# A mixture of experts behind cross attention: expert tiles of 128 rows, each with its own expert, two to a group

## The chip, the cores and the metric

The kernel runs on one core of one Trainium2 chip. The metric is the time on the device in microseconds (us). TensorE's granted clock has two levels, 1.2 and 2.4 GHz; the profile shows it as 0.50 and 1.00. The profile's engines are PE (TensorE's matmuls), PEld (its weight loads), DVE, ACT, POOL and SP; a name with a q behind it (PEldq, SPq, ACTq, POOLq) is the engine's queue, its sequencer, which runs register instructions, waits and DMA issues. A read of a value from memory into a register is a TENSOR_LOAD there.

## The reference

The input is x, 32 x 256 tokens of 256 numbers (8192 tokens), and a context of the same shape, all in float32.

```
x = x + xattn(layernorm(x), ctx)          # 8 heads of 64, both directions, mixed by alpha
h = layernorm(x)                          # 8192 x 256
probs = softmax(h @ gate_w.T)             # 16 experts
w, idx = top_k(probs, 4); w /= sum(w)
g, u = h @ w1[e], h @ w3[e]               # 256 -> 128 each, per expert
y[e] = (silu(g) * u) @ w2[e]              # 128 -> 256
x = x + sum over the 4 chosen e of w[e] * y[e]
```

So 8192 x 4 = 32768 rows go through an expert, each through one of 16.

## The kernel before, in words

**Stage A** takes the 32 batches one after another: layer norm, projections, scores, softmax, attention, output projection, second layer norm, router. For each chosen expert of each token it sends the normed row by an indirect DMA of POOL into `x_rows`, a table in HBM with a region for each expert; behind the row's 256 numbers lies the row's place in the result `y_rows`. A matrix is held as a high and a low part, and each product is made of three passes (hi x hi, hi x lo, lo x hi: `PASSES`).

**The plan.** When the last batch is routed, DVE counts the rows of each expert (`count`), the groups that they fill (`over` is a comparison of 16 experts with `MOST` fill levels, `ngroups` its sum), and makes a table: for each group its row in `x_rows` and its expert. SP stores it and reads it back as `table_row`. SP and ACT write a pad behind each expert's rows, one group long, eight experts each (`pad_experts`, `pad`, lines 349 and 350): bias rows, and targets in a dump region behind `y_rows`. One more pad of one group for each of 16 unused groups is written in stage A.

**The expert stage** works on 144 groups of 256 rows (two tiles of 128 rows, n = 0 and 1, of the same expert). 144 is 32768 / 256 = 128 full groups and one partly filled for each of 16 experts. The order on each engine is written out by hand as a pipeline over the body of group j, r = j mod 8. The first and the last eight groups are unrolled, the rest is a loop whose body holds eight groups.

- SP (`load_group`, lines 419 and 420) reads the group's row from `table_row` into a register and loads 256 rows into one of eight buffers `xg`. For a buffer's next use it waits for the transposes of the group eight back, and for that group's sends.
- PE, in body j: reloads the expert of group j - 2 where r is 0 or 1 (the registers don't live across the loop's jump); transposes the rows of group j + 1 (line 1202, `p_xt`); reads the expert of j (line 1189); gate and up matmuls of j (line 1213, `p_gu`, 12 matmuls of 256 columns, whose weights are addressed by the expert's register); transposes the activations of j - 1 (line 1223, `p_at`); down matmuls of j - 2 (line 1231, `p_y`, 6 matmuls).
- ACT, in body j: tanh of j - 1 (line 663), copy of `p_at` of j - 2 (668), copy of `p_y` of j - 3 to `y_out` (673), copy of `p_xt` of j + 1 to `xgT_hi` (678). DVE does the products of silu (939, 942) and the low parts (948, 954).
- POOL sends the two tiles of `y_out` row by row to their places in `y_rows` by two indirect DMAs (line 524).

Two buffers lie between the steps (`p_xt`, `xgT`, `p_gu`, `gated`, `p_at`, `actT`, `p_y`), four for `y_out`, eight for `xg`. Line 43 is the helper that waits for a semaphore.

**The end**: when all sends have landed, SP loads the rows of `y_rows` and the residual, DVE weights and sums them, and ACT stores the result.

Of the kernel before, what the change touches and what calls it, by code (L numbers as in the profile page):

```python
# [6 lines left out]
F32 = mybir.dt.float32  # L7
F32R = mybir.dt.float32r
U32 = mybir.dt.uint32
I32 = mybir.dt.int32  # L10
# [5 lines left out]
P = 128  # L16
TOP_K = 4
# [10 lines left out]
def flat(ap):  # L28

    names = " ".join("abcd"[:len(ap.shape) - 1])  # L30
    return ap.rearrange(f"p {names} -> p ({names})")


def spread(ap, axis, shape):

    return ap.unsqueeze(axis).to_broadcast(shape)
# [9 lines left out]
def xattn_moe_kernel(nc, x, ctx, Wq1, Wk1, Wv1, Wq2, Wk2, Wv2, alpha_attn, Wout, bout,  # L46
# [12 lines left out]
    SCALE = HEAD_DIM ** -0.5  # L59
    TOKENS = B * S  # L60
    TT = TOKENS // P
    GROUP = 2 * P

    REGION = TOKENS + GROUP
    ROW = D + 4

    GROUPS = TOKENS * TOP_K // GROUP + E
    MOST = TOKENS // GROUP
    DUMP = TOKENS * TOP_K
    PIECE = KT * INNER  # L70
    LOADS = 8
    TC = -(-GROUPS // P)
    assert S == 2 * P and D == 2 * P and INNER == 4 * P and I == P and B >= 4 and B % 4 == 0
    assert math.frexp(SCALE)[0] == 0.5
    assert GROUPS % LOADS == 0 and GROUPS >= 3 * LOADS
    ROUTER_STEPS = 19

    x_rows = nc.dram_tensor("x_rows", [E * REGION + E * GROUP, ROW], F32, kind="Internal").ap()
    y_rows = nc.dram_tensor("y_rows", [DUMP + 2 * E * GROUP, D], F32, kind="Internal").ap()
    mid_rows = nc.dram_tensor("mid_rows", [TOKENS, D], F32, kind="Internal").ap()  # L80
    group_table = nc.dram_tensor("group_table", [2, TC * P], I32, kind="Internal").ap()

    with ExitStack() as stack:
        def sb(name, shape, dt=F32, stack=stack):
            return stack.enter_context(nc.sbuf_tensor(name, shape, dt))
# [32 lines left out]
        with ExitStack() as a:  # L118


            qT = [[sb(f"qT{d}_{part}", [P, PAIRS, S], F32R, a) for part in ("hi", "lo")] for d in range(2)]
            kT = [[sb(f"kT{d}_{part}", [P, PAIRS, S], F32R, a) for part in ("hi", "lo")] for d in range(2)]
            wp = [sb("wp_hi", [P, 6, KT, INNER], F32R, a), sb("wp_lo", [P, 6, KT, INNER], F32R, a)]
            gate_rows = sb("gate_rows", [E, D], stack=a)
            val = [sb(f"val{d}", [P, ST, INNER], stack=a) for d in range(2)]
            rows = sb("rows", [P, ST, D], stack=a)

            rowsT = [[sb(f"rowsT{i}_{part}", [P, KT, S], F32R, a) for part in ("hi", "lo")] for i in range(2)]
            x_in = sb("x_in", [P, ST, D], stack=a)
            x_res = sb("x_res", [P, ST, D], stack=a)  # L130
            x_mid = sb("x_mid", [P, ST, D], stack=a)
            probs = [sb(f"probs{i}", [P, 2, ST, S], stack=a) for i in range(2)]
            probsT = sb("probsT", [P, 2, ST, S], stack=a)
            attnT = sb("attnT", [P, PAIRS, S], stack=a)
            moeT = [sb("moeT_hi", [P, KT, S], F32R, a), sb("moeT_lo", [P, KT, S], F32R, a)]
            routed = sb("routed", [P, ST, TOP_K, ROW], stack=a)
            middle_slots = [sb(f"middle_slot{i}", [P, PIECE], stack=a)[:, :] for i in range(2)]
            pad_target = sb("pad_target", [P, 2 * E, 2], I32, a)
            small = lambda name, shape, dt=F32: sb(name, shape, dt, a)
            nmx, sums, inv = ([small(f"{n}{i}", [P, 4]) for i in range(2)] for n in ("nmx", "sums", "inv"))  # L140
            stats = small("stats", [P, ST, 6])
            mv = small("mv", [P, ST, 2])
            ve = small("ve", [P, ST])
            rstd = small("rstd", [P, ST])
            lmax = small("lmax", [P, ST])
            lexp = small("lexp", [P, ST, E])
            pexp = small("pexp", [P, ST, E])
            top = small("top", [P, ST, 8])
            topi = small("topi", [P, ST, 8], U32)
            topf = small("topf", [P, ST, TOP_K])  # L150
            tsum = small("tsum", [P, ST])
            trec = small("trec", [P, ST])
            onehot = small("onehot", [P, ST, TOP_K, E])
            chosen = small("chosen", [P, ST, E])
            chosen_b = small("chosen_b", [P, ST, E], BF16)
            place = small("place", [P, ST, E])
            slotf = small("slotf", [P, ST, TOP_K])
            slot_i = small("slot_i", [P, ST, TOP_K], I32)
# [184 lines left out]

            return not isinstance(j, int) or 0 <= j < GROUPS

        def pad(eng, row, n, groups):

            to = x_rows[bass.ds(row, groups * GROUP), :].rearrange("(n p) d -> p n d", p=P)
            eng.dma_start(to[:, :, 0:D], spread(bias[:, :], 1, [P, 2 * groups, D])).then_inc(pads_sent, 16)
            eng.dma_start(to[:, :, D:D + 1].bitcast(I32), flat(pad_target[:, n:n + groups, :]).unsqueeze(2),  # L350
                          allow_slow_non_contiguous=True).then_inc(pads_sent, 16)

        def pad_experts(eng, experts):
# [7 lines left out]
        def _(sp):  # L361
# [54 lines left out]
            sp.wait_ge(table_in, 16)  # L416

            def load_group(j, r):
                row = sp.value_load(table_row[0:1, 0, bass.ds(j, 1)], min_val=0, max_val=E * REGION + (E - 1) * GROUP)
                sp.dma_start(xg[r][:, :, 0:D + 1],  # L420
                             x_rows[bass.ds(row, GROUP), 0:D + 1].rearrange("(n p) d -> p n d", p=P)).then_inc(xg_in[r], 16)

            for r in range(LOADS):
                load_group(r, r)
# [24 lines left out]
        def _(pool):  # L449
            for t in (ident, before, ones, routed):  # L450
# [5 lines left out]

            pool.affine_select(out=before[:, :], in_=before[:, :], compare_op=ALU.is_gt, fill=0.0,
                               base=0, pattern=[[1, P]], channel_multiplier=-1).then_inc(consts_set, 1)
            pool.iota(pad_target[:, :, :], [[GROUP, 2 * E], [P, 2]], base=DUMP, channel_multiplier=1).then_inc(consts_set, 1)
            pool.memset(mhalf[:, :], -0.5).then_inc(consts_set, 1)  # L460
            for t, pattern, start, mult in (
                    (expert[:, :], [[1, E]], 0, 0),
                    (region[:, :], [[REGION, E]], 0, 0),
                    (base[:, :], [[REGION, E]], 0, 0),
                    (target[:, :, :], [[P * TOP_K, ST], [1, TOP_K]], 0, TOP_K),
                    (fills[:, :], [[GROUP, MOST]], 0, 0),
                    (tri[:, :, :], [[1, E], [-1, E]], 0, 0),
                    (group_no[:, :], [[P, TC]], 0, 1)):
                pool.iota(t, pattern, base=start, channel_multiplier=mult,
                          allow_small_or_imprecise_dtypes=True).then_inc(consts_set, 1)  # L470
# [225 lines left out]
        def _(dve):  # L696
# [205 lines left out]
            def planned(ins):  # L902
                n_steps[0] += 1
                ins.then_inc(plan_step, 1)
                dve.wait_ge(plan_step, n_steps[0])
# [14 lines left out]
            planned(dve.tensor_tensor(tstart[:, :], group_no[:, :], tstart[:, :], ALU.subtract))  # L920
            planned(dve.tensor_scalar(trow[:, :], texp[:, :], float(REGION), None, ALU.mult))
            planned(dve.tensor_copy(base_i[:, :], base[:, :]))
            planned(dve.scalar_tensor_tensor(trow[:, :], tstart[:, :], float(GROUP), trow[:, :], ALU.mult, ALU.add))

            dve.tensor_scalar(table[:, 1, :], texp[:, :], float(E - 1), None, ALU.min)
            planned(dve.tensor_copy(table[:, 0, :], trow[:, :]))
# [52 lines left out]
        def _(pe):  # L979
# [205 lines left out]
            pe.wait_ge(middle_hi, MIDDLE)  # L1185
            pe.wait_ge(late_lo, LATE)

            def expert_of(j):
                return pe.value_load(table_row[0:1, 1, bass.ds(j, 1)], min_val=0, max_val=E - 1)

            experts = {}

            def group(j, r):
                if exists(j - 2) and r < 2:
                    experts[(r - 2) % LOADS] = expert_of(j - 2)
                if exists(j + 1):
                    i = (r + 1) % 2
                    pe.wait_ge(xg_in[(r + 1) % LOADS], xg_loads(j + 1, r + 1))
# [4 lines left out]
                    mm.then_inc(xg_t, 1)  # L1203
                if exists(j):
                    i = r % 2
                    experts[r] = expert_of(j)
                    pe.wait_ge(xgT_lo, j + 1)
                    wait(pe, act_set, j - 1)
                    for n in range(2):
                        m = 0  # L1210
                        for k in range(KT):
                            for h, a in PASSES:
                                mm = pe.matmul(p_gu[:, i, n, :], xgT[i][h][:, n, k, :],  # L1213
                                               wgu[a][:, bass.ds(experts[r], 1), k, :, :].rearrange("p e g i -> p (e g i)"),
                                               start=(m == 0), stop=(m == 5))
                                m += 1
                    mm.then_inc(gu_done, 1)
# [7 lines left out]
                if exists(j - 2):  # L1225
                    i = r % 2
                    pe.wait_ge(actT_lo, j - 1)
                    wait(pe, y_set, j - 3)
                    for n in range(2):
                        for m, (h, a) in enumerate(PASSES):  # L1230
                            mm = pe.matmul(p_y[:, i, n, :], actT[i][h][:, n, :],  # L1231
                                           wdn[a][:, bass.ds(experts[(r - 2) % LOADS], 1), :].rearrange("p e d -> p (e d)"),
                                           start=(m == 0), stop=(m == 2))
                    mm.then_inc(down_done, 1)

            def xg_loads(j, r):

                return 16 // LOADS * (j - r % LOADS) + 16

            stage_b(pe, group, before=1, after=2)  # L1240

# [24 lines left out]
```

## Time and profile before

| | us |
|---|---|
| median of three runs | 2395.33 (2387.25 to 2414.63) |
| the profiled execution, its time | 2383.63 |
| its span, first to last instruction | 2381.8 |
| PE busy in the span | 1987.9 (83%) |
| DVE, ACT, POOL busy | 1407.4, 1259.3, 1228.2 |
| mean granted clock of TensorE | 0.954 |

How to read it: the profile's times count from the first instruction. Stage A lasts until about 1678, the expert stage's matmuls lie between 1713 and 2228, the final sums behind 2236. Busy time of an engine is what its instructions take; register instructions, waits and DMA issues of the queues are not in it. "issue" in the chain of waits is time in which an engine waited for nothing that the profile shows; "remote" and "another core or an unknown queue" stand for a releaser that it could not find. The starts of the matmuls are measured, their ends modelled.

### The profile page before, as it was taken

The numbers are of one execution on the slowest core, as the hardware profiler recorded it, in microseconds if no ns is written. First come the engines' busy times: TensorE is split into PE (matmuls) and PEld (weight loads), VectorE is DVE, ScalarE is ACT, GpSimd is POOL, SyncE is SP. The second block draws the span as 40 slices with busy tenths as digits, with TensorE's granted clock in tenths as the row PEclk, the third lists the DMA queues.
The fourth block names the chain that finished last, engine by engine and source line by source line (L and its number), as shares of the span: only waits on it lengthen the run. The fifth ranks groups of instructions, "written<-read, shape, count | busy, mean of one in ns | idle before, by whom it ended". The sixth has DMA issues, their size and how long they took to land.

```text
span 2381.8 us, 53628 instructions
## 1 busy us (share of the span) xinstructions
PE 1987.9 (83%) x15906; PEld 1664.9 (70%) x15907; DVE 1407.4 (59%) x3173; ACT 1259.3 (53%) x3605; POOL 1228.2 (52%) x1683
## 2 busy tenths in 40 slices
PE   6999999999999999999999999997288888888300
PEld 5777777777777777777777777775287777777300
DVE  4665666666666666666666666664545544455477
ACT  5755566655666655666655666654144444444200
POOL 2465556665555665555665555664255555555300
PEclk9999999999999999999999999999599999999755
DMA  5411100111100111100011000112854444554699
GB/s 153 121 41 49 36 31 31 33 40 47 36 31 31 33 41 46 36 31 31 33 42 49 31 31 31 36 43 77 187 149 146 149 145 148 148 147 142 216 359 331
DMA packets 158596, 210.54 MB, mean 88 GB/s; under 512 B 24273, under 2 KB 131425, under 8 KB 158562
## 3 DMA queue, kind: packets, MB, share of 16 engines
q1 hardware_dynamic: 119394, 127.75, 18.5%
q0 software_dynamic: 26112, 71.86, 8.5%
q10 hardware_dynamic: 13056, 10.50, 1.5%
q8 instruction: 18, 0.29, 0.1%
q14 instruction: 16, 0.13, 0.0%
HBM read 113.02 MB, written 97.03 MB: 88 GB/s over the span
## 4 chain that ended last, share of the span: by engine, by line
PE 62%; DVE 9%; ACT 9%; issue 8%; DMA 6%; another core or an unknown queue 3%; SPq 1%; POOL 1%; DVEq 0%; ACTq 0%; POOLq 0%
PE p_s L1003 12%; PE p_pt L1067 11%; PE p_av L1081 11%; PE p_gu L1213 8%; ACT probs L583 5%; PE p_s L1051 5%; PE p_av L1096 5%; PE p_s L1013 3%; PE p_y L1231 3%; DVE nmx L800 3%; DMA z<-mid_rows 3%; PE p_xt L1202 2%; DMA out_dram<-z 2%; ACT val L553 1%
## 5 line engine op out<-in xcount | busy, mean ns | idle before, releaser
L488 POOL TENSOR_TENSOR probs<-probs,inv 128x256 f32<-128x256 f32 x1024 | 599.5, 618 | 485.2 <-DVE inv L807 484.1
L583 ACT ACTIVATE probs<-p_s,nmx 128x256 f32<-128x256 f32 x1024 | 473.0, 479 | 56.7 <-DVE nmx L800 47.5
L524 POOL DMA_INDIRECT y_rows<-y_out,xg x288 | 277.1, 962 | 270.5 <-ACT y_out L673 203.1
L800 DVE TENSOR_REDUCE nmx<-p_s 128x4 f32<-128x1024 f32 x256 | 312.7, 1221 | 36.7 <-PE p_s L1051 35.9
L1003 PE MATMUL p_s<-rowsT_hi,wp_hi 128*128 128x256 f32 x896 | 268.3, 299 | 49.1 <-DVE rowsT_lo L811 45.4
L480 POOL DMA_INDIRECT x_rows<-routed,slot_i x256 | 261.0, 1019 | 79.2 <-issue 68.1
L1067 PE MATMUL p_pt<-ident,probs 128*128 128x128 f32 x2048 | 281.3, 279 | 9.4 <-ACT val L553 9.2
L1067 PEld LDWEIGHTS p_pt<-ident,probs 128*128 128x128 f32 x2048 | 220.2, 141 | 94.0 <-POOL probs L488 46.7
L1081 PE MATMUL p_av<-probsT,val 128*64 128x256 f32 x2048 | 277.5, 391 | 5.6 <-DVE probsT L708 2.5
L708 DVE COPY probsT<-p_pt 128x512 f32<-128x512 f32 x256 | 176.1, 688 | 164.6 <-PE p_pt L1067 161.9
L1003 PE MATMUL p_s<-rowsT_lo,wp_hi 128*128 128x256 f32 x896 | 253.5, 283 | 0.0
L1003 PE MATMUL p_s<-rowsT_hi,wp_lo 128*128 128x256 f32 x896 | 253.4, 283 | 0.0
L1213 PE MATMUL p_gu<-wgu_hi,xgT_hi 128*128 x576 | 175.9, 305 | 66.4 <-DVE xgT_lo L954 38.5
L1003 PEld LDWEIGHTS p_s<-rowsT_hi,wp_hi 128*128 128x128 f32 x896 | 171.1, 191 | 74.7 <-ACT probs L583 49.5
L583 ACT ACTIVATION_READ_ACCUMULATOR probs<-p_s,nmx 128x1 f32 x1024 | 213.9, 209 | 0.0
L954 DVE TENSOR_TENSOR xgT_lo<-p_xt,xgT_hi 128x512 fp32r<-128x512 f32 x144 | 99.0, 687 | 181.2 <-ACT xgT_hi L678 175.9
L571 ACT COPY probsT<-p_pt 128x512 f32<-128x512 f32 x256 | 150.6, 588 | 71.1 <-PE p_pt L1067 67.8
L1081 PEld LDWEIGHTS p_av<-probsT,val 128*64 128x64 f32 x2048 | 130.6, 136 | 72.2 <-issue 9.4
L1051 PE MATMUL p_s<-kT_hi,qT_hi 64*128 64x256 f32 x1024 | 171.0, 330 | 6.4 <-DVE qT_lo L823 6.4
L1003 PEld LDWEIGHTS p_s<-rowsT_lo,wp_hi 128*128 128x128 f32 x896 | 171.5, 191 | 1.2
L1003 PEld LDWEIGHTS p_s<-rowsT_hi,wp_lo 128*128 128x128 f32 x896 | 171.2, 191 | 0.0
L1213 PEld LDWEIGHTS p_gu<-wgu_hi,xgT_hi 128*128 128x128 f32 x576 | 109.6, 190 | 85.7 <-issue 85.2
(176 smaller groups left out, 4673.6 us busy)
## 6 DMA issues: line engine op xcount, KB each, us to landing
xg<-x_rows SPq DMA_DIRECT2D x144, 257.0 KB
y_in<-y_rows SPq DMA_DIRECT2D x32, 1024.0 KB, 6.4
rows<-in_ctx_dram SPq DMA_DIRECT2D x32, 256.0 KB
x_in<-in_x_dram SPq DMA_DIRECT2D x32, 256.0 KB, 2.6
mid_rows<-x_mid SPq DMA_DIRECT2D x32, 256.0 KB
z<-mid_rows SPq DMA_DIRECT2D x32, 256.0 KB, 7.4
out_dram<-z ACTq DMA_DIRECT2D x32, 256.0 KB, 5.9
y_rows<-y_out,xg POOLq DMA_INDIRECT x288
```

The lines of the kernel that those rows point to most:

```text
L480: pool.indirect_dma_start(x_rows, bass.IndirectOffsetOnAxis(ap=slot_i[:, t, k:k + 1], axis=0), routed[:, t, k, :], None).then_inc(rows_sen ...
L488: pool.tensor_tensor(pr[:, h, t, :], pr[:, h, t, :], rc[:, g:g + 1].to_broadcast([P, S]), ALU.mult).then_inc(normed_p, 1)
L524: pool.indirect_dma_start(y_rows, bass.IndirectOffsetOnAxis(ap=xg[r][:, i, D:D + 1].bitcast(I32), axis=0), y_out[r % 4][:, i, :], None).th ...
L571: act.copy(flat(probsT[:, 0, :, :]), p_pt[:, 0, :]).then_inc(pt_out_a, 1)
L583: act.activation(probs[u % 2][:, h, t, :], p_s[:, 2 * (u % 2) + h, t * S:(t + 1) * S], ACT.Exp, bias=nmx[u % 2][:, g:g + 1], accum_out=sum ...
L708: dve.tensor_copy(flat(probsT[:, 1, :, :]), p_pt[:, 1, :]).then_inc(pt_out_b, 1)
L800: dve.tensor_reduce(nmx[i][:, :], p_s[:, 2 * i:2 * i + 2, :].rearrange("p h (t k) -> p (h t) k", t=ST), AX.X, ALU.max, negate=True).then_i ...
L1003: mm = pe.matmul(proj_bank(n)[:, j * S:(j + 1) * S], wp[a][:, w, k, c:c + P], rowsT[w // 3][r][:, k, :], start=(i == 0), stop=(i == 5))
L1051: mm = pe.matmul(p_s[:, 2 * d + h, t * S:(t + 1) * S], qT[d][q][r:r + HEAD_DIM, p, t * P:(t + 1) * P], kT[d][k][r:r + HEAD_DIM, p, :], sta ...
L1067: mm = pe.transpose(p_pt[:, h, k * S + t * P:k * S + (t + 1) * P], probs[u % 2][:, h, t, k * P:(k + 1) * P], ident[:, :])
L1081: mm = pe.matmul(p_av[r:r + HEAD_DIM, 0:S], val[d][:, k, c:c + HEAD_DIM], probsT[:, h, k, :], start=(d == 0 and k == 0), stop=(d == 1 and ...
L1213: mm = pe.matmul(p_gu[:, i, n, :], xgT[i][h][:, n, k, :], wgu[a][:, bass.ds(experts[r], 1), k, :, :].rearrange("p e g i -> p (e g i)"), st ...
```

## The change

A tile of 128 rows gets an expert and a place in `x_rows` of its own. The plan counts tiles, not groups of 256 rows: 32768 / 128 + 16 = 272 tiles, and two in sequence of the table make a group, so there are 136 groups. `MOST` becomes 64 for 32, `TC` 3 for 2. Pads are one tile long for each expert, in both places where they are written. SP reads two rows of the table for a group and issues two loads of 128 rows; both raise the buffer's semaphore. PE reads two experts where it read one, and the weights of the matmuls of n = 0 and n = 1 are addressed by different registers. ACT, DVE and POOL keep their work in a group; the buffers stay.

```diff
-    GROUP = 2 * P
-    REGION = TOKENS + GROUP
+    PAIR = 2
+    REGION = TOKENS + P
-    GROUPS = TOKENS * TOP_K // GROUP + E
-    MOST = TOKENS // GROUP
+    TILES = TOKENS * TOP_K // P + E
+    GROUPS = TILES // PAIR
+    MOST = TOKENS // P
-    TC = -(-GROUPS // P)
+    TC = -(-TILES // P)
...
-        def pad(eng, row, n, groups):
+        def pad(eng, row, n, tiles):
-            to = x_rows[bass.ds(row, groups * GROUP), :].rearrange("(n p) d -> p n d", p=P)
+            to = x_rows[bass.ds(row, tiles * P), :].rearrange("(n p) d -> p n d", p=P)
...
             def load_group(j, r):
-                row = sp.value_load(table_row[0:1, 0, bass.ds(j, 1)], ...)
-                sp.dma_start(xg[r][:, :, 0:D + 1],
-                             x_rows[bass.ds(row, GROUP), 0:D + 1].rearrange("(n p) d -> p n d", p=P)).then_inc(xg_in[r], 16)
+                for n in range(PAIR):
+                    row = sp.value_load(table_row[0:1, 0, bass.ds(PAIR * j + n, 1)], ...)
+                    sp.dma_start(xg[r][:, n, 0:D + 1], x_rows[bass.ds(row, P), 0:D + 1]).then_inc(xg_in[r], 16)
...
-            def expert_of(j):
-                return pe.value_load(table_row[0:1, 1, bass.ds(j, 1)], min_val=0, max_val=E - 1)
+            def experts_of(j):
+                return [pe.value_load(table_row[0:1, 1, bass.ds(PAIR * j + n, 1)], min_val=0, max_val=E - 1)
+                        for n in range(PAIR)]
...
                 if exists(j - 2) and r < 2:
-                    experts[(r - 2) % LOADS] = expert_of(j - 2)
+                    experts[(r - 2) % LOADS] = experts_of(j - 2)
...
-                    experts[r] = expert_of(j)
+                    experts[r] = experts_of(j)
...
-                                               wgu[a][:, bass.ds(experts[r], 1), k, :, :].rearrange("p e g i -> p (e g i)"),
+                                               wgu[a][:, bass.ds(experts[r][n], 1), k, :, :].rearrange("p e g i -> p (e g i)"),
...
-                                           wdn[a][:, bass.ds(experts[(r - 2) % LOADS], 1), :].rearrange("p e d -> p (e d)"),
+                                           wdn[a][:, bass.ds(experts[(r - 2) % LOADS][n], 1), :].rearrange("p e d -> p (e d)"),
...
-                return 16 // LOADS * (j - r % LOADS) + 16
+                return 16 * PAIR // LOADS * (j - r % LOADS) + 16 * PAIR
```

## Rows read from the trace of the kernel before

**Rows 1.** Table of windows: stretch; its length, busy us (instructions) by engine; clock, DMA share, GB/s

```profile
1740.00:2200.00 460.00, 385.19 (x3072) 360.74 (x3071) 227.88 (x511) 215.40 (x512) 246.23 (x256) 1.00 0.50 147
```

**Rows 2.** Line 1213, expert stage: count; shortest/median/longest ns; first and last start

```profile
L1213 PE MATMUL p_gu<-wgu_hi,xgT_hi x576: 277/280/574, 1713.4 to 2223.3; 128*128 x192
```

**Rows 3.** Line 1231, the down matmuls, same stage and columns

```profile
L1231 PE MATMUL p_y<-wdn_hi,actT_lo x288: 276/281/415, 1720.9 to 2227.7; 128*128 x144
...
L1231 PEldq FUSED_REGOPS  x144: 46/46/46, 1720.3 to 2226.9; - x144
L1231 PEldq ALU_OP  x144: 32/32/32, 1720.4 to 2227.0; - x144
```

**Rows 4.** Timeline of PE, 1719 to 1729: start, us; first gate-up matmul of two groups

```profile
1721.74 0.36 PE L1213 MATMUL p_gu<-wgu_hi,xgT_hi 128*128 x1
...
1724.52 0.36 PE L1213 MATMUL p_gu<-wgu_hi,xgT_hi 128*128 x1
```

**Rows 5.** Chain of waits in order of time, 1823 to 1840: start, us, what

```profile
1823.40 1.68 PE p_gu L1213 x12
...
1826.44 0.27 issue
...
1830.40 1.69 PE p_gu L1213 x12
...
1836.14 0.60 ACT xgT_hi L678
...
1837.60 1.68 PE p_gu L1213 x12
```

**Rows 6.** Table of waits, 1740 to 2200: us in total, times, longest

```profile
ACT y_out L673 <- remote: 114.4, 50, 2.7
```

**Rows 7.** Timeline of POOL, 1819 to 1831; in brackets the idle time before

```profile
1822.73 0.96 POOL L524 DMA_INDIRECT y_rows<-y_out,xg  x1 [2.37 <-ACT y_out L673]
...
1826.53 0.96 POOL L524 DMA_INDIRECT y_rows<-y_out,xg  x1 [0.30 <-issue]
1829.82 0.96 POOL L524 DMA_INDIRECT y_rows<-y_out,xg  x1 [2.33 <-ACT y_out L673]
```

**Rows 8.** Line 1189, PE's value loads, 1824.6 to 1828.6

```profile
L1189 PEldq TENSOR_LOAD <-table_row x3: 296/356/393, 1824.8 to 1827.8; - x3
```

**Rows 9.** The same line, 1825.6 to 1827.6, the middle one of these three

```profile
L1189 PEldq FUSED_REGOPS  x2: 46/98/151, 1825.6 to 1826.1; - x2
L1189 PEldq TENSOR_LOAD <-table_row x1: 296/296/296, 1825.8 to 1825.8; - x1
L1189 PEldq SEQ_ASSERT  x1: 18/18/18, 1826.3 to 1826.3; - x1
```

**Rows 10.** Line 1213's register instructions, 1824.6 to 1828.6, before one group's matmuls

```profile
L1213 PEldq FUSED_REGOPS  x2: 46/46/46, 1826.6 to 1826.8; - x2
L1213 PEldq ALU_OP  x2: 32/32/32, 1826.7 to 1827.0; - x2
```

**Rows 11.** Line 1189 right behind the loop's jump, 1820.5 to 1821.6

```profile
L1189 PEldq TENSOR_LOAD <-table_row x1: 537/537/537, 1820.7 to 1820.7; - x1
```

**Rows 12.** Chain of waits, 1640 to 1725: pads and the first loads

```profile
1682.01 4.74 SPq L349
...
1700.34 6.60 DMA x_rows<-pad_target
...
1707.89 0.41 SPq L420
...
1709.08 3.12 DMA xg<-x_rows
```

**Rows 13.** Costliest groups of instructions, 1672 to 1679: the plan on DVE; busy us, mean ns

```profile
L910 DVE TENSOR_TENSOR over<-count,fills 128x512 f32<-128x512 f32 x1 | 0.8, 768 | 0.0
...
L914 DVE TENSOR_TENSOR trin<-tri,ngroups 128x256 f32<-128x256 f32 x1 | 0.4, 427 | 0.0
```

**Rows 14.** Line 524, POOL's sends, expert stage

```profile
L524 POOL DMA_INDIRECT y_rows<-y_out,xg x288: 957/963/971, 1723.0 to 2233.8; - x144
```

More of the change, by code:

```diff
@@ L76, in xattn_moe_kernel @@
     ROUTER_STEPS = 19
-    x_rows = nc.dram_tensor("x_rows", [E * REGION + E * GROUP, ROW], F32, kind="Internal").ap()
-    y_rows = nc.dram_tensor("y_rows", [DUMP + 2 * E * GROUP, D], F32, kind="Internal").ap()
+    x_rows = nc.dram_tensor("x_rows", [E * REGION + E * P, ROW], F32, kind="Internal").ap()
+    y_rows = nc.dram_tensor("y_rows", [DUMP + 2 * E * P, D], F32, kind="Internal").ap()
     mid_rows = nc.dram_tensor("mid_rows", [TOKENS, D], F32, kind="Internal").ap()
@@ L137, in xattn_moe_kernel @@
             middle_slots = [sb(f"middle_slot{i}", [P, PIECE], stack=a)[:, :] for i in range(2)]
-            pad_target = sb("pad_target", [P, 2 * E, 2], I32, a)
+            pad_target = sb("pad_target", [P, 2 * E], I32, a)
             small = lambda name, shape, dt=F32: sb(name, shape, dt, a)
@@ L344, in exists @@
             return not isinstance(j, int) or 0 <= j < GROUPS
-        def pad(eng, row, n, groups):
-            to = x_rows[bass.ds(row, groups * GROUP), :].rearrange("(n p) d -> p n d", p=P)
-            eng.dma_start(to[:, :, 0:D], spread(bias[:, :], 1, [P, 2 * groups, D])).then_inc(pads_sent, 16)
-            eng.dma_start(to[:, :, D:D + 1].bitcast(I32), flat(pad_target[:, n:n + groups, :]).unsqueeze(2),
+        def pad(eng, row, n, tiles):
+            to = x_rows[bass.ds(row, tiles * P), :].rearrange("(n p) d -> p n d", p=P)
+            eng.dma_start(to[:, :, 0:D], spread(bias[:, :], 1, [P, tiles, D])).then_inc(pads_sent, 16)
+            eng.dma_start(to[:, :, D:D + 1].bitcast(I32), pad_target[:, n:n + tiles].unsqueeze(2),
                           allow_slow_non_contiguous=True).then_inc(pads_sent, 16)
@@ L418, in load_group @@
             def load_group(j, r):
-                row = sp.value_load(table_row[0:1, 0, bass.ds(j, 1)], min_val=0, max_val=E * REGION + (E - 1) * GROUP)
-                sp.dma_start(xg[r][:, :, 0:D + 1],
-                             x_rows[bass.ds(row, GROUP), 0:D + 1].rearrange("(n p) d -> p n d", p=P)).then_inc(xg_in[r], 16)
+                for n in range(PAIR):
+                    row = sp.value_load(table_row[0:1, 0, bass.ds(PAIR * j + n, 1)], min_val=0,
+                                        max_val=E * REGION + (E - 1) * P)
+                    sp.dma_start(xg[r][:, n, 0:D + 1], x_rows[bass.ds(row, P), 0:D + 1]).then_inc(xg_in[r], 16)
             for r in range(LOADS):
@@ L458, in _ @@
                                base=0, pattern=[[1, P]], channel_multiplier=-1).then_inc(consts_set, 1)
-            pool.iota(pad_target[:, :, :], [[GROUP, 2 * E], [P, 2]], base=DUMP, channel_multiplier=1).then_inc(consts_set, 1)
+            pool.iota(pad_target[:, :], [[P, 2 * E]], base=DUMP, channel_multiplier=1).then_inc(consts_set, 1)
             pool.memset(mhalf[:, :], -0.5).then_inc(consts_set, 1)
@@ L465, in _ @@
                     (target[:, :, :], [[P * TOP_K, ST], [1, TOP_K]], 0, TOP_K),
-                    (fills[:, :], [[GROUP, MOST]], 0, 0),
+                    (fills[:, :], [[P, MOST]], 0, 0),
                     (tri[:, :, :], [[1, E], [-1, E]], 0, 0),
@@ L922, in _ @@
             planned(dve.tensor_copy(base_i[:, :], base[:, :]))
-            planned(dve.scalar_tensor_tensor(trow[:, :], tstart[:, :], float(GROUP), trow[:, :], ALU.mult, ALU.add))
+            planned(dve.scalar_tensor_tensor(trow[:, :], tstart[:, :], float(P), trow[:, :], ALU.mult, ALU.add))
             dve.tensor_scalar(table[:, 1, :], texp[:, :], float(E - 1), None, ALU.min)
```

## The prediction, made before the changed kernel was run

> **What bounds the kernel now.** I read the table of windows first, to find the stage that the change touches: from 1740 to 2200 us TensorE is busy 385 of 460 us at the full clock (1.00, the 2.4 GHz level), POOL 246, DVE 228, ACT 215, and the DMA engines half the time, so no unit is full [rows 1]. Then the two lines of the expert matmuls: 144 groups lie between the first gate-up matmul at 1713.4 and the last down matmul at 2227.7, 514.3 us or 3.57 us a group [rows 2, 3]. Without disturbance the array needs less: at the stage's start, before POOL sends anything, one group follows the next in 2.78 us [rows 4]. So 0.8 us of each group is waiting. The chain of waits shows the rhythm: the groups come in pairs, one pair from 1830.40 to 1837.60, and a pair ends with a wait for the transposed rows (ACT's copy at 1836.14, with DVE's rest behind it) [rows 5]. The table of waits names the delay ahead of that copy: ACT stands idle before y_out for 114 us in all, 2.7 us at most, for something that the profile cannot name [rows 6]. POOL meanwhile sends four times in a row (1822.73, and so on to 1826.53), and then stands 2.33 us until the next y_out [rows 7]. The pair of groups, four sends, one hold-up, is the clock of this stage: 7.1 us.
>
> The last place I looked at is TensorE's queue, the sequencer that reads registers ahead of the array, because the change edits it. In two bodies of the loop out of eight (r of 0 and 1) the expert of two groups back is loaded again. Around 1825 this queue is the one that is late: the array stands idle 0.27 us for "issue" at 1826.44 [rows 5], while the queue goes through three value loads between 1824.6 and 1828.6 [rows 8]. That stretch prices the queue with hardly a wait in it.
>
> **The prices on TensorE's queue.** Value loads begin at 1825.8 and 1827.8, at the same place of two successive bodies [rows 8, 9]: a body with one value load takes about 2.05 us (2.0 by these starts; the instructions behind the second begin slightly later). The load itself, from its index at 1825.6 to its last check at 1826.3 and the step to the next instruction, takes 0.8 us, though the read proper takes 0.30 [rows 9]. A reload in a body costs 1.0 (1824.8 to 1825.8) [rows 8, 9]. The addresses of one group's gate-up matmuls (two weight tensors, two k's) are four register instructions; they begin at 1826.6, 1826.7, 1826.8 and 1827.0, 0.12 us apiece [rows 10]. Those of the down matmuls are two: one of each kind, 144 times for 144 groups [rows 3]. The first load behind the loop's jump takes 0.54 in place of 0.30 [rows 11].
>
> **The change part by part.** *Gone: 8 of 144 groups.* At today's pace 8 x 3.57 = 28.6 us, if the pace holds. The number of matmuls, evacuations and sends in a group stays, so the array's 2.78 and POOL's two sends stay.
>
> *Added in TensorE's queue:* each group has two experts. One more value load, 0.8. The matmuls of n = 1 take their weights at other registers, so the four and two address instructions double: 6 x 0.12 = 0.7. A body becomes 2.05 + 0.8 + 0.7 = 3.55. The reload in two bodies of eight becomes 1.0 + 0.8 = 1.8, or 0.45 a body; the jump is worth 0.05. Together 4.05 us a body, against 2.05 + 0.25 + 0.05 = 2.35 now. Today that lies hidden beside the array (2.78) and the pair's rhythm (3.57); at 4.05 it is over both, and nothing is left to hide it: a queue that works in order cannot be overtaken. 136 x 4.05 = 551, and some 3 for the two bodies that drain: 554 for 514, so +40. What I cannot see is how often this queue will still stand at a semaphore: 0 if everything that it waits for has a whole body to arrive, and up to 0.3 a body (41 us) if the hold-ups stay, since in the pair at 1825 the array's idle was 0.27 [rows 5]. I take 0, because the slower bodies give each partner more time, and keep 41 for the range. The other bound is that the doubled addresses are not there or cost nothing (0.7 x 136 = 95 less on the queue, in which case other limits take over, see below).
>
> Of this the Trainium skill says in "DMA: Bandwidth & Descriptors", section "Latency and other measured facts", that a tensor_load has a floor of about 600 ns. The trace disagrees: 296 to 393 ns here [rows 8, 9], and only behind the jump 537 [rows 11]. By the page the 1.25 further loads a body would cost 0.3 more each, 51 us over the stage; the sum goes by the rows.
>
> *Added in SP's queue:* a second value load and DMA per group. Two loads at the start are 1.19 apart (1707.89, 1709.08) [rows 12], so a group takes 2.4, under 3.57 and 4.05: hidden, and if that cover went (a group under 2.5 us) the loads would come late. It does cost at the start, where the first matmuls wait for the first two groups: group 0 is complete 1.2 later and group 1 2.4 later, less 0.3 for smaller transfers: +1.5.
>
> *Plan on DVE*, on the path, since the table and the pads wait for it: the comparison and its sum go from 512 to 1024 elements. the nearest rows, 427 ns for 256 elements and 768 for 512, put 512 more at 0.68 [rows 13], and the sum behind it at about as much: +1.3.
>
> *Pads.* Each expert's pad is 128 rows, not 256: 2.1 MB in place of 4.2. The last one's little transfer lands 6.60 us after its issue, a queue of bytes, while a load then needs 3.12 [rows 12]: -3.5. The one stall of SP's queue, 4.74 at 1682, lies in the same crowd [rows 12]; half the bytes may save between 0 and all of it, I take -2. The issues themselves are as many as before.
>
> *End.* After the last down matmul at 2227.7 POOL still sends, the last time from 2233.8 for 0.96 [rows 3, 14], since the last groups come faster than 2.5 us. Slower bodies leave less behind: -2 (0 to -3). The final sums read the same bytes.
>
> Sum: +40 + 1.5 + 1.3 - 3.5 - 2 - 2 = +35. The profiled execution took 2383.6 (span 2381.8), 11.7 under the median of the three runs, 2395.3. On it the changed kernel takes 2419; told against the median, 2430.
>
> **Rivals.**
> *A, the pair keeps its rhythm* (faster). The queue's new work fits behind the array after all, and each pair takes 7.1 again. For it: today the pair with the two reloads is no longer than the next (1823.40 to 1830.40, 7.0, against 7.2) [rows 5]. Against it: that one needs 2 x 2.05 + 2 x 1.0 + 0.4 = 6.5, which fits in 7.1; two plain new bodies alone make 7.1, and the two with reloads 11. It needs a body under 3.57 on average. Price: -28.6 and the -5 of the ends: 2362.
> *B, in between* (no change). The addresses don't double in time, so plain bodies take 2.9 and hide, but the pair with reloads takes 2 x 2.85 + 3.6 + 0.4 = 9.7 for 7.1. Eight bodies take 31.0, 136 take 527: +13 - 5 = +8, 2403. It decides from a plain pair under 7.1.
> *C, both* (slower still). The queue is the bound and still stands at the held-up semaphores, 0.3 a body: +76, 2471. A lower granted clock in the array's longer pauses would look alike; today it stays at 1.00 in 83% busy [rows 1], and it would be 68%.
> That the change doesn't do what it says (136 groups not enough, so nothing removed) is excluded: 16 partly filled tiles beside 256 full ones are 272.
>
> **The numbers.** Forecast 0.50, A 0.20, B 0.18, C 0.12. A per cent (24 us) is about what this kernel's measurement can tell. Slower by over 1%: C and most of the forecast, 0.57. Within: B and the forecast's low edge, 0.23. Faster: A, 0.20. The range goes from A's middle, 2360, to C with a little above, 2478: some 15 in 100 lie outside.
>
> **What would show it.** TensorE's value loads: 272 and the reloads, two behind each other 0.8 apart; eight address instructions for gate-up and four for down; a loop of eight groups in 32 us for 28.5; the array idle for "issue" ahead of the gate-up matmuls, 1 to 1.3 us a group; POOL's sends no longer four in a row; pads landing within 3 us. Pairs of 7.1 us, or bodies at 3.6, would make the prediction wrong, in that the queue's work was no bound; address rows unchanged in number would make B right.

## The result, and the profile after

The changed kernel takes 2433.7 us (median of 4 runs, 2432.1 to 2437.5) beside 2397.5 of the kernel before (4 runs): a ratio of 1.0154, 95% interval [1.0118, 1.0190]. Forecast: 2430, slower. On another chip, used later, the same change costs more than three times as much (ratio 1.0549). That is the most important thing that the experiments found, and the prediction knew nothing of it.

The profiled execution after took 2437.5 us (span 2435.8), the one before 2383.6: 53.9 apart, since the one before lay 14 under its median.

Table of windows, 1740 to 2200 us, the kernel after (columns as in [rows 1]): no unit has become full, all have become emptier (the order is PE, PEld, DVE, ACT, POOL). TensorE went from 385 to 352 busy us.

```profile
1740.00:2200.00 460.00, 352.26 (x2612) 322.81 (x2611) 201.55 (x434) 189.23 (x435) 206.83 (x215) 0.96 0.42 123
```

The expert lines of after (columns as in [rows 2, 3]). 136 groups now lie between 1710.2 and 2279.7, 569.5 us for 514.4. The register instructions are eight a group for the gate-up matmuls (544 + 544 over 136) and four for the down matmuls:

```profile
L1216 PEldq FUSED_REGOPS  x544: 3/46/661, 1710.1 to 2273.4; - x182
...
L1216 PE MATMUL p_gu<-wgu_hi,xgT_hi x544: 279/283/579, 1710.2 to 2274.0; 128*128 x182
L1216 PEldq ALU_OP  x544: 3/32/71, 1710.2 to 2273.6; - x182
...
L1234 PEldq FUSED_REGOPS  x272: 16/46/51, 1717.4 to 2279.2; - x136
L1234 PEldq ALU_OP  x272: 5/32/32, 1717.6 to 2279.3; - x136
...
L1234 PE MATMUL p_y<-wdn_hi,actT_lo x272: 276/283/415, 1718.1 to 2279.7; 128*128 x136
...
L1191 PEldq TENSOR_LOAD <-table_row x340: 3/302/729, 1708.6 to 2278.2; - x170
```

FUSED_REGOPS and ALU_OP are the register instructions, the last line is the value loads: 340 are 272 (two a group) and 68 reloads. Their longest times, 661 and 729 ns, are stalls of this queue.

The table of waits, 1740 to 2200, shows who waits for what (us in total, times, longest). TensorE waits for "issue", its own queue, ahead of the gate-up matmuls: 101 us on the side of the weight loads (PEld) and 47 on that of the matmuls (PE). The two run side by side and their idle times overlap, so they can't be added. The matmuls stand idle 460 - 352 = 108 us in all, 1.0 a group over the 108 groups of this window: 47 for the queue ahead of the gate-up matmuls, 28 for it ahead of the transposes, and 29 put down to DVE. The wait of y_out for something unnamed [rows 6] is gone, but 88 us of the same kind stand ahead of the gate.

```profile
POOL y_rows L526 <- ACT y_out L675: 204.1, 74, 5.3
DVE gated L941 <- ACT gated L665: 156.5, 74, 3.6
PEld p_gu L1216 <- issue: 101.3, 97, 1.7
...
ACT gated L665 <- remote: 87.8, 27, 3.9
...
PE p_gu L1216 <- issue: 47.1, 56, 1.4
...
PE p_gu L1216 <- DVE gated L944: 28.6, 38, 1.2
PE p_xt L1205 <- issue: 27.5, 22, 2.2
```

The timeline of POOL still has four sends in a row ([rows 7]), but less often. Between 1740 and 2200 the kernel before has 59 runs of four sends and none of two; after has 31 runs of four and 41 of two (a run ends where POOL waits over 1 us). Here a run of four, a pair, and the send behind it:

```profile
1891.28 0.96 POOL L526 DMA_INDIRECT y_rows<-y_out,xg  x1 [1.96 <-ACT y_out L675]
1892.56 0.96 POOL L526 DMA_INDIRECT y_rows<-y_out,xg  x1 [0.32 <-issue]
1893.84 0.96 POOL L526 DMA_INDIRECT y_rows<-y_out,xg  x1 [0.32 <-issue]
1895.10 0.97 POOL L526 DMA_INDIRECT y_rows<-y_out,xg  x1 [0.30 <-issue]
...
1906.81 0.96 POOL L526 DMA_INDIRECT y_rows<-y_out,xg  x1 [3.03 <-ACT y_out L675]
1908.07 0.96 POOL L526 DMA_INDIRECT y_rows<-y_out,xg  x1 [0.30 <-issue]
1911.21 0.96 POOL L526 DMA_INDIRECT y_rows<-y_out,xg  x1 [2.18 <-ACT y_out L675]
```

The chain of waits of after through the pads and first loads (compare [rows 12]; start, us, what). The stall of 4.74 us in SP's queue is gone, and two of 1.50 and 0.93 are there; the last small pad transfer takes as long as before, 6.61:

```profile
1686.98 1.50 SPq L351
...
1689.75 0.93 SPq L351
...
1695.52 6.61 DMA x_rows<-pad_target
```

And the plan's comparison and its sum, twice as wide (columns as in [rows 13]):

```profile
L912 DVE TENSOR_TENSOR over<-count,fills 128x1024 f32<-128x1024 f32 x1 | 1.3, 1299 | 0.0
L914 DVE TENSOR_REDUCE ngroups<-over 128x16 f32<-128x1024 f32 x1 | 1.2, 1220 | 0.0
```

**The 53.9 us between the two profiles.** Up to the first gate-up matmul 3.1 less (1713.4, 1710.2); the stage 55.1 more; from the last down matmul to the first load of the final sums 1.7 less (8.7, 7.0); the final sums to the end 3.6 more (145.4, 149.0). The last is no effect of the change: one and the same kernel, profiled twice later, took 145.8 and 150.6 us there.

### The profile page after: what moved, and what is told of

Its sections match the earlier page's. It is cut to its first block, busy times and chain, and to the rows that moved or that the text cites. A ratio compares the mean times of both kernels' runs of the same rounds, so it can differ in the third digit from the quotient of the medians.

```text
span 2435.8 us, 55300 instructions
## 1 busy us (share of the span) xinstructions
PE 1993.9 (82%) x15714; PEld 1661.8 (68%) x15715; DVE 1403.3 (58%) x3141; ACT 1254.0 (51%) x3573; POOL 1211.6 (50%) x1667
## 4 chain that ended last, share of the span: by engine, by line
PE 63%; issue 10%; ACT 8%; DVE 8%; DMA 5%; another core or an unknown queue 2%; SPq 2%; POOL 1%; DVEq 0%; ACTq 0%; POOLq 0%
PE p_s L1005 12%; PE p_pt L1069 11%; PE p_av L1083 11%; PE p_gu L1216 8%; ACT probs L585 5%; PE p_s L1053 5%; PE p_av L1098 5%; PE p_s L1015 4%; PE p_y L1234 3%; DVE nmx L802 3%; DMA z<-mid_rows 3%; PE p_xt L1205 2%; DMA out_dram<-z 2%; ACT val L555 1%
## 5 line engine op out<-in xcount | busy, mean ns | idle before, releaser
L526 POOL DMA_INDIRECT y_rows<-y_out,xg x272 | 261.6, 962 | 337.0 <-ACT y_out L675 267.8
L665 ACT ACTIVATE gated<-p_gu 128x256 f32<-128x256 f32 x136 | 52.6, 387 | 247.3 <-PE p_gu L1216 119.8
L941 DVE SCALAR_TENSOR_TENSOR gated<-gated,p_gu 128x256 f32<-128x256 f32 x136 | 57.2, 421 | 208.4 <-ACT gated L665 183.2
```

The source lines that it names most:

```text
L526: pool.indirect_dma_start(y_rows, bass.IndirectOffsetOnAxis(ap=xg[r][:, i, D:D + 1].bitcast(I32), axis=0), y_out[r % 4][:, i, :], None).th ...
```

## The experiments

Two theories from the start. **Queue:** TensorE's queue has 4.05 us of work a body and sets the pace. **Rival:** something else of the change does, such as the doubled loads. In the numbers below "a loop" is the time from one jump of the loop on TensorE's queue to the next, eight groups; its mean was 28.8 us before and 33.9 after. The first four kernels ran on one chip, where the kernel before took 2395.7 us (18 runs), about as on the chip of the result. "Before" and "after" stand for the two kernels.

**One expert a pair.** After, with the queue of before: one value load and one register for both tiles. The other engines' instructions are those of after.

```
-                return [pe.value_load(table_row[0:1, 1, bass.ds(PAIR * j + n, 1)], ...) for n in range(PAIR)]
+                e = pe.value_load(table_row[0:1, 1, bass.ds(PAIR * j, 1)], min_val=0, max_val=E - 1)
+                return [e, e]
```

> The changed kernel, but TensorE reads one expert a group (that of the first tile) and uses its register for both tiles, so second tiles whose expert differs get the wrong weights. TensorE's queue has the work of the kernel before; groups, pads, plan and SP's loads are those of the changed one. Queue theory: the loop falls back to the pair rhythm, 28.5 us for eight groups, the stage takes about 486 us, and the time is 2397 - 28.6 - 4 = about 2365. Rival (the stage is slow for another reason of the change, such as SP's two loads a group): 2434 as the changed kernel.

Measured: 2384.5 us, ratio 0.9952 [0.9925, 0.9978]. The loss is gone with the queue's work: the stage takes 514.9 us for 569.5. But the gain that 8 groups fewer should bring is not there in full: a loop takes 30.4 us in the mean (mostly 30.6 to 30.8), 1.6 more than before. The last two take 28.7 and 28.6, though SP still loads then (its last load goes out at 2209.8, the last of these loops ends at 2187).

**Two loads, one used.** As above, but the second value is loaded and left unused, so only the six address instructions are missing.

```
+                e = [pe.value_load(... PAIR * j + n ...) for n in range(PAIR)]
+                return [e[0], e[0]]
```

> The changed kernel with both value loads in TensorE's queue, but the matmuls of both tiles take the first one's register (second tiles with another expert get the wrong weights), so the six further address instructions are gone. Queue theory: a plain body is 3.55 - 0.7 = 2.85 us and hides, only the pair with reloads is over 7.1 (about 9.7): 31 us for eight groups, about 2403. If addresses cost nothing: 2434. If only the addresses count and value loads hide anyway: 2365.

Measured: 2407.9 us, 1.0051 [1.0027, 1.0076], 32.1 us a loop. The second load adds 1.7 us to a loop, and the six addresses another 1.8 (to 33.9): each of the two terms counts. The addresses of a loop are 8 x 0.72 = 5.8 us of queue work, so taking them out gave back a third of it; then other waits of this chip take over, near the 31 us that the expectation gives for them.

**The kernel before with two registers.** 144 groups of 256 rows, SP untouched, but the expert is loaded twice and each half has its own register: TensorE's queue of after and nothing else of it.

```
-                return pe.value_load(table_row[0:1, 1, bass.ds(j, 1)], min_val=0, max_val=E - 1)
+                return [pe.value_load(table_row[0:1, 1, bass.ds(j, 1)], min_val=0, max_val=E - 1) for n in range(2)]
...
-                                               wgu[a][:, bass.ds(experts[r], 1), k, :, :]
+                                               wgu[a][:, bass.ds(experts[r][n], 1), k, :, :]
```

> The kernel before with its 144 groups of one expert, but TensorE reads the group's expert twice into two registers and addresses the second tile's matmuls by the second one; the output is that of the kernel before. Queue theory: eight groups take 33.9 us as in the changed kernel, the stage 144 x 33.9 / 8 = 610 for 514, the time about 2397 + 90 = 2487. Rival (something else in the change is what costs): 2397.

Measured: 2454.2 us, 1.0252 [1.0229, 1.0275]. The rival of no effect falls. The whole came out 33 us under the expectation; a loop takes 32.4 us (31.9 to 33.4), the prediction's 8 x 4.05, and not the 33.9 of after. Its lines (columns as before) show 144 groups from 1715.2 to 2294.9, 579.7 us:

```profile
L1214 PE MATMUL p_gu<-wgu_hi,xgT_hi x576: 277/280/578, 1715.2 to 2289.9; 128*128 x192
...
L1232 PE MATMUL p_y<-wdn_hi,actT_lo x288: 276/281/415, 1723.3 to 2294.9; 128*128 x144
```

**One read of two values.** After, with one register read that fetches both experts, without the check of their bounds. The addresses stay doubled.

```
+                return nc.values_load_multi_w_load_instructions(
+                    table_row[0:1, 1, bass.ds(PAIR * j, PAIR)], engines=[PE], min_val=0, max_val=E - 1,
+                    skip_runtime_bounds_check_because=...)[1]
```

> The changed kernel with the two experts of a group read by one register load of two values, and without the run-time check of their bounds; the computation is the same. Queue theory: the read takes 0.45 in place of 1.6 us, a body 3.55 - 1.15 = 2.4 (reload bodies 2.9), all hidden, so the pair rhythm returns with 136 groups: about 2365, faster than both kernels. If the queue is not the bound: 2434. If a read of two values costs as much as two reads: about 2410, by the missing checks alone.

Measured: 2386.2 us, 0.9957 [0.9942, 0.9971], 30.6 us a loop: as fast as the one with one expert, whose queue has 4.05 - 2.35 = 1.7 us a body less to do than after's. So something else is the limit at 30.6.

**What is the limit left over?** SP's waits gave the hint that was followed. In 1740 to 2100 of the kernel with one expert a pair, the table shows hardly a wait of SP for transfers:

```profile
SPq L421 <- DMA y_rows<-y_out,xg: 2.1, 3, 0.8
```

It is busy or stalled nearly all the time. But the same trace has what speaks against SP: in this window the rows of all 93 groups have landed 1.8 us or more (in the middle 3.8) before TensorE begins to transpose them, so no group waited for SP's loads. The next kernels followed the hint all the same. Three kernels were to tell SP's reads from the mere number of transfers, and one to see whether the queues bound the kernel before: after with one read of two values on *both* queues (e7); before with one read but two transfers of 128 rows (e8); before with the row read twice (e9); before without bounds checks (e10).

```
 e7   at = one unchecked read of both rows, then the two dma_start
-e8   sp.dma_start(xg[r][:, :, 0:D + 1], x_rows[bass.ds(row, GROUP), 0:D + 1]...)
+e8   for n in range(2): sp.dma_start(xg[r][:, n, 0:D + 1], x_rows[bass.ds(row + n * P, P), 0:D + 1])
-e9   row = sp.value_load(...)
+e9   row = [sp.value_load(...) for n in range(2)][1]
 e10  both value loads of before with skip_runtime_bounds_check_because=...
```

After with one read on both queues:

> The kernel with one unchecked read of two values on TensorE's queue, and now the same on SP's: one unchecked read gives both tiles' rows, then the two loads. Theory Q (SP's queue is what is left: in the kernel with one expert a pair, SP waits for transfers only 2.1 us in 300, so its 3.84 us a body set the 30.7 us per loop of 8; the second read with its bounds check takes about 0.8 us of that): 3.84 - 0.5 or more puts SP under the 3.56 us of the kernel before, a loop takes 28.5 to 29.2 us, 1.6 us less, over 15 loops 24 us less than the 2386 of one unchecked read on TensorE alone: 2362. Theory D (two transfers a group cost by themselves, whatever the reads do): 30.6 us per loop, 2386.

Before with two transfers:

> The kernel before with one read of the group's row on SP's queue and two transfers of 128 rows in place of one of 256. Theory Q: only one issue of 0.38 us is added to SP's queue, whose body grows from 3.25 us of work (28.5 us per loop less 2.5 of waiting, over 8) to 3.63: 29.0 us per loop, +0.5, over 17 loops +9 us: 2405. Theory D: the loop takes the 30.7 us that it takes in the changed kernel with one expert a pair, +2.1 us, over 17 loops +35 us: 2431.

Before with two reads:

> The kernel before with the group's row read twice on SP's queue, the second value used; one transfer as before. Theory Q: 0.80 us a body more on SP's queue, 3.25 + 0.80 = 4.05 us, which is over the 3.56 us that a body takes now: up to 32.4 us per loop if the queue's stalls stay, no less than the 30.7 of the changed kernel with one expert a pair, so +2.1 to +3.9 us over 17 loops: 2433 to 2463. Theory D: the number of transfers is that of before, 28.5 us per loop, 2397.

Before unchecked:

> The kernel before with the bounds checks taken out of both reads of the table (0.20 us of register work and assertion on SP's queue for each, about as much on TensorE's). If the rhythm of before is set by late semaphores and by GpSimd's sends and no queue of register work bounds it: 28.5 us per loop, 2397. If TensorE's queue bounds it: 0.20 us less a body, 1.6 us less per loop, over 18 loops 29 us: 2368. If it is SP's, whose waits for transfers are 2.5 of 28.5 us, at most the same 29 us.

Measured, on a second chip: the kernel before itself took 2288.4 us there (25 runs), 107 less than on the first, so no absolute time of these expectations could come true. Ratios: e7 0.9967 [0.9956, 0.9979] at 2280.7 us, e8 0.9982 [0.9969, 0.9995], e9 1.0004 [0.9994, 1.0015], e10 0.9956 [0.9940, 0.9972] at 2278.2. Neither another read nor another transfer on SP costs anything here. Without the bounds checks a loop of the kernel before takes 22.5 us, beside 23.1 with the row read twice. The question that they were made for, reads or transfers, needs the first chip and stays open. But a greater one came up: why is the expert stage of the kernel before some 96 us shorter here? With the row read twice it takes 418.1 us (514.4 on the first chip), 23.1 a loop, and the stage begins at 1713.0 as on the first (1713.4).

**The same again, with after itself,** on a third chip (before: 2284.0 us, 19 runs). The kernels are unchanged.

> The changed kernel as it is, beside the kernel before, because the kernel before took 2288 us on the last chip and 2397 on the one ahead of it, with 22.9 and 28.5 us per loop of 8 groups in the expert stage and nothing else different. Theory: TensorE's queue of the changed kernel is 4.05 us a body on any chip, while the kernel before's 28.5 us holds semaphore updates up to 2.8 us late that the second chip does not have. If this run is on a chip where before takes about 2288: 32.4 us per loop, 9.5 more than before, over 17 loops +160 us: 2448, ratio 1.07. If it is on one where before takes about 2397: 33.9 us per loop and 2434, ratio 1.015, as seen. Rival (the change costs about 1.5% on every chip): 2324 on the one, 2434 on the other.

> The changed kernel with one unchecked read of two values on TensorE's queue and on SP's, again. Where before takes about 2288 it should repeat 24.7 us per loop and 2281. Where before takes about 2397: theory Q (SP's queue is what kept one read on TensorE alone at 30.7 us per loop): 28.5 to 29.2 us per loop, 2362; theory D (two transfers a group cost by themselves): 30.6 us per loop, 2386.

> The kernel before with the row read twice on SP's queue, again. Where before takes about 2288, SP has time to spare and it should again be no different: 22.9 us per loop, 2288. Where before takes about 2397: theory Q, SP's queue full of stalls, 30.7 us per loop or more, +2.1 over 17 loops: 2433; theory D, 28.5 us per loop, 2397.

Measured: after 2410.2 us, ratio 1.0549 [1.0532, 1.0567]; the two others repeat, 0.9974 [0.9963, 0.9984] and 1.0005 [0.9995, 1.0015]. The rival (1.5% on every chip) falls. After takes 32.7 us a loop, 4.09 a body, beside the 4.05 of the sum; in the mean a plain body takes 3.7 us (3.55 forecast) and the two with reloads 10.8 together (11.1). The value loads in TensorE's queue, one body at 1901.5 to 1903.3 of this run (line, operation, count, ns min/median/max, starts), are 0.8 apart:

```profile
L1191 PEldq FUSED_REGOPS  x4: 46/106/151, 1901.7 to 1902.9; - x4
L1191 PEldq SEQ_ASSERT  x3: 18/18/18, 1901.5 to 1903.1; - x3
L1191 PEldq TENSOR_LOAD <-table_row x2: 298/298/299, 1901.8 to 1902.6; - x2
```

The windows of 1740 to 2100 on this chip, first after, then the kernel before with the row read twice. The latter is what the kernel before can do when nothing disturbs it: TensorE 98% busy, 2.89 us a group.

```profile
1740.00:2100.00 360.00, 282.86 (x2108) 261.14 (x2106) 164.42 (x352) 154.64 (x352) 167.98 (x176) 0.96 0.43 128
```

```profile
1740.00:2100.00 360.00, 353.36 (x2987) 347.39 (x2986) 232.36 (x498) 214.35 (x498) 238.26 (x250) 1.00 0.61 182
```

On the first chip the kernel before has, in the same window, TensorE 301 us busy. Its table of waits there, and that of the kernel with two reads on the third chip:

```profile
DVE xgT_lo L954 <- ACT xgT_hi L678: 137.1, 51, 3.8
POOL y_rows L524 <- ACT y_out L673: 118.3, 51, 2.5
ACT y_out L673 <- remote: 110.0, 48, 2.7
```

```profile
POOL y_rows L525 <- issue: 98.8, 226, 2.1
ACT gated L664 <- PE p_gu L1214: 97.5, 112, 1.5
DVE gated L940 <- ACT gated L664: 68.9, 124, 1.2
DVE xgT_lo L955 <- ACT xgT_hi L679: 54.4, 125, 1.2
...
POOL y_rows L525 <- ACT y_out L674: 23.2, 24, 1.2
```

"Remote", the releaser that the profile can't name, is there on the first chip and nowhere in the table on the third. The semaphore events of the traces say what it is. From 1800 to 2080 us of the kernel before on the first chip, half of TensorE's updates for the transposed rows (78 matmuls) come 1.55 us or more after the start of their matmul, up to 2.48. (Three would be at 4.2 to 6.0, but some records of updates are missing, and these may be the next group's.) On the third chip, in the kernel with two reads, 9 in 10 come after 0.29, and in after all four kinds of TensorE's updates come within 0.44. The queues stall too. The checks of SP's value load, same window, with one expert a pair on the first chip, and with two reads on the third (ns min/median/max):

```profile
L421 SPq SEQ_ASSERT  x188: 3/18/704, 1740.1 to 2099.8; - x188
```

```profile
L419 SPq SEQ_ASSERT  x249: 18/18/18, 1740.4 to 2099.3; - x125
```

An instruction of 18 ns takes up to 704 on the one and always 18 on the other.

**Fewer waits.** After with single reads takes 24.6 us a loop on the undisturbed chips, where the kernel before unchecked does 22.5. Why? The trace tells where: from one group's first gate-up matmul to the next, six of eight groups take 2.8 us, the pace of the array, and only the two bodies with reloads take mostly 3.8 to 4.0. If it is TensorE's queue in these two, taking anything out of it helps. Three waits per group repeat what the group before has waited for already, and go.

```
-                    wait(pe, xgT_lo, j)
-                    wait(pe, act_set, j - 1)
-                    wait(pe, actT_lo, j - 2)
```

> The changed kernel with one unchecked read of two values on both queues, and without three waits per group on TensorE's queue that the group before has already made (for the conversion ahead of the transposes of x, for the product of the gate, for the conversion of the transposed product). Theory (where no update is held, TensorE's queue still bounds that kernel: 24.7 us per loop, 3.08 a body, against the array's 2.81): three semaphore instructions of 0.12 us less give 2.72 a body, so the array's 2.81 sets it: 22.5 to 22.9 us per loop, 2.0 less over 17 loops, -31 us: where the kernel before takes about 2286, 2278 - 31 = 2247, ratio 0.983. Rival (24.7 us is the work's own round trip through ScalarE and VectorE and not the queue): no change, 24.7 us per loop, 2278, ratio 0.997. Where the kernel before takes about 2397 its rhythm is that of the late updates and neither is told apart.

Measured, on a fourth chip, where the kernel before took 2451.3 us: 2411.2, ratio 0.9836 [0.9822, 0.9849]. It beats the kernel before, and with it the changed one, which lost to it on both chips where they met. That chip is of the disturbed sort (44 us of "remote" ahead of the gate in 1740 to 2100; 30.8 us a loop; a stage of 520.9), for which the expectation said that the theories aren't told apart. They aren't: the kernel before wasn't profiled there and the same kernel with the three waits in it wasn't run, so how much the waits give is open.

## Why the prediction came true, and where it did not

*TensorE's queue* (+40): the mechanism is shown. A body of 4.05 us was forecast, 32.4 a loop. The kernel before with only this edit takes 32.4, after on an undisturbed chip 32.7, and without the doubled loads and addresses the loss is gone. The kernel before with this edit alone loses 2.5%, more than the whole change. Rival A needed a body under 3.57 us, rival B addresses that cost nothing; they cost 1.8 us a loop. The value load at 0.8 us and the address at 0.12 could be read from one busy stretch [rows 8 to 10]. The Trainium skill's floor of about 600 ns for a tensor_load ("DMA: Bandwidth & Descriptors", section "Latency and other measured facts") isn't borne out: 298 ns above, and the loops agree with the sum by the rows. Of the signs that it named, the counts and the 0.8 us came, and the loop of 32 us as 33.9. The idle time for "issue" ahead of the gate-up matmuls is 0.4 us a group of the array's and not 1 to 1.3, since part of its idle time, 1.0 in all, stands elsewhere. POOL's four sends in a row became fewer and did not go: on the chip of the result the hold-ups go on beside the queue.

*The time a queue stands at semaphores* (taken as 0, bound 41) and *SP's second load* (taken as hidden): together mis-sized. After on the chip of the result takes 33.9 a loop, 1.5 more than the sum, and the stage 569.5 for 554. With TensorE's queue the same and SP's as before it is 32.4, so these 1.5 come with the doubled loads (the other differences, plan and pads, lie ahead of the stage); on the undisturbed chip only 0.3 of it is left. SP's cover of "2.4 us under 3.57" counted its instructions as they run freely, and stalls of 0.7 us are in them here. Yet hidden was right in so far as no load was late: in after the rows lie ready 2.9 us or more before their transposes (83 groups, 1740 to 2100, in the middle 7.1). By which way the loads cost 1.5 a loop is open.

*What the kernel before was bound by*: the step that failed. "The pair of groups, four sends, one hold-up, is the clock of this stage" took the hold-up for a trait of the kernel. The kernel's own pace stood in [rows 4], 2.78 us a group, and an unnamed releaser in [rows 6]. On two of four chips there is no hold-up, POOL sends twice as its rows come, and a group takes 2.9 us. So 8 groups are worth 23 us and not 28.6 there, and the new queue costs 4.09 - 2.89 = 1.2 us in each of 136 groups: 163 less 23, 140. Stages of 550.0 and 418.1 us say 132, the measured times 126. The forecast was near because it was made and measured where the kernel before was slowed already: the hold-ups hid most of the queue's work. That is luck, as nothing in the prediction asked for a chip of that sort.

*The start.* Plan: +1.0 (5.1 to 6.1 us from its first instruction to the table) for +1.3. Pads: from the table to the last landing 28.6 us before, 22.3 after, -6.3 for -5.5, but not as said. "Landing within 3 us" is wrong, 6.61 is unchanged, so that term of -3.5 was 0; the pads are issued in 14.3 us instead of 20.6, since not only the stall of 4.74 shrank: five of 0.7 us behind it are gone. The chain of before:

```profile
1686.80 0.68 issue
...
1687.49 0.69 issue
1688.18 0.70 SPq L350
1688.88 0.70 issue
...
1689.58 0.70 issue
```

The same stalls of 0.7 us as in the stage, on a chip that has them. The first loads: +1.7 for +1.5. *The end:* -1.7 for -2. The small sums hold; the two pad terms were right only together.

*The totals.* +35 was forecast between profiles and 53.9 came; between medians 36.2 came. The 15 us of the stage that were missing and the 3.6 of the final sums were offset by the profile of before lying under its median. So the closeness of 2430 to 2433.7 is in part luck.

## What to carry to other kernels

In these traces a dynamic index costs TensorE's queue 0.8 us to load with its check and 0.12 us for every address made from it. Before a change that adds indices, sum the queue's work per iteration against the busiest unit's time and not against the iteration as it is now: what looks like slack may be a disturbance that another chip doesn't have. One read for several values, without bounds checks where the data can't break them, was 0.3 to 0.4% faster than the kernel before on one disturbed chip (on TensorE's queue alone) and on two undisturbed ones (on both queues); the changed kernel itself lost 5.5% on one of these two. And where the profile has a releaser that it can't name, compare with a stretch without it, or another chip, ahead of explaining the rhythm by the kernel.

## What the runs showed of the hardware

Four chips gave the kernel before two paces: 2284 and 2288 us on two, 2396 and 2451 on two others. On the slow ones semaphore updates from TensorE come microseconds late (in the kernel before up to 3.1 us after the start of their matmul, beside 0.29 on the fast ones), and instructions of SP's queue that are 18 ns long take 700. On the fourth chip some 28 us more are lost ahead of the expert stage (its first gate-up matmul starts at 1734.4 with fewer waits, at 1706.6 with one read on the first chip). In the stage of the kernel before the first late update is that of a matmul at 1725.9, 2.9 us after POOL's first indirect send (1723.0, [rows 14]); before it they come within 0.43. The last late one comes at 2223.6, some 10 us after SP's last load is issued (2212.7), while POOL sends until 2233.8. That fits the two streams together on these chips, though not to the microsecond at the end; no run changed one of them alone there, so the cause is open. Each chip was used in one stretch of time only, so it isn't shown either that the chip makes the difference and not something else that ran beside the kernel.

The mean granted clock was 0.96 in the stage after, for 1.00, on the slow and the fast chip alike, with TensorE busy 77 and 79%. It is a mean of the two levels: the clock stands at 2.4 GHz for most of the stage and falls to 1.2 for short stretches again and again, where the kernel before has one such stretch. It came with the array's longer pauses: at 83% busy, with one expert a pair, it was 0.99. Since the queue sets the pace, no loss of time is put down to it here, and no run tells it apart.
